# Row maxima turned by one transpose per phase, the image loop written out, and a 4-bit weight decoded inside the first image

## What is computed

```python
h = group_norm(x, 8 groups) * w + b
q, k, v = split(qkv_w @ h + qkv_b)             # one head of 128
x = x + proj_w @ (softmax(q k^T / sqrt(128)) v) + proj_b
t = tokens(x)                                  # 1024 x 128
n = layer_norm(t)
sq, sk, rq = n @ wq_s / 4, n @ wk_s, n @ wq_r / 4    # 8 heads of 16
retrieved = softmax(sq sk^T) @ (n @ wv_r)      # for each of 2 retrievers
t = t + mix(softmax(rq . (retrieved @ wk_ret)), retrieved) @ w_out
W4 = NF4_TABLE[qidx] * scales                  # 128 x 128, blocks of 16
t = t + layer_norm(t) @ W4^T @ W^T
```

## Time and profile before

| what | value |
|---|---|
| median of 3 runs | 4804.96 us (4800.92 to 4805.71) |
| profiled execution, its own time | 4802.95 us |
| its span (first to last instruction) | 4801.1 us |
| mean granted TensorE clock | 0.986 |
| instructions in it | 102107 |
| busy: PE, POOL, DVE, ACT | 96%, 88%, 81%, 69% |
| bytes moved by DMA | 191.77 MB, mean 40 GB/s |

### The profile page before, as it was taken

One profiled execution on the slowest core, in us unless ns is written; L12 is line 12 of the kernel. 1 busy time (PEld: TensorE's weight loads), 2 busy tenths in 40 slices (PEclk: granted clock), 3 DMA queues, 4 the chain that ended last, 5 costly groups with the idle time before them and its releaser, 6 DMA issues.

```text
span 4801.1 us, 102107 instructions
## 1 busy us (share of the span) xinstructions
PE 4608.7 (96%) x29838; PEld 2533.9 (53%) x29838; DVE 3906.7 (81%) x8190; ACT 3317.4 (69%) x6657; POOL 4242.2 (88%) x1142
## 2 busy tenths in 40 slices
PE   5899999999999999999999999999999999999985
PEld 4555555555555555555555555555555555555532
DVE  4788888888888888888888888888888888888863
ACT  2567777777777777777767777767777777777654
POOL 1589999999999999999999999999999999999996
PEclk9899999999999999999999999999999999999987
DMA  1011111111111111111111111111111111111010
GB/s 33 23 45 45 50 32 45 32 45 45 49 32 45 32 45 45 49 32 45 32 45 45 49 32 45 32 45 46 49 32 46 31 45 49 45 32 49 24 40 14
DMA packets 92739, 191.77 MB, mean 40 GB/s; under 512 B 16744, under 2 KB 50920, under 8 KB 92400
## 3 DMA queue, kind: packets, MB, share of 16 engines
q1 hardware_dynamic: 92400, 186.45, 13.9%
HBM read 17.53 MB, written 16.78 MB: 7 GB/s over the span
## 4 chain that ended last, share of the span: by engine, by line
PE 85%; DVE 6%; ACT 4%; issue 3%; POOL 1%; SPq 0%; DVEq 0%; ACTq 0%; DMA 0%; POOLq 0%
PE ps_u L804 18%; PE ps_bank L769 13%; PE ps_bank L791 11%; PE ps_bank L755 10%; PE ps_bank L741 4%; PE ps_bank L679 4%; DVE max_part L1067 4%; PE ps_bank L690 3%; PE ps_bank L710 3%; ACT p L962 3%; PE ps_bank L813 3%; PE ps_bank L743 3%; PE ps_bank L744 2%; PE ps_bank L742 2%; DVE max_part L1051 2%
## 5 line engine op out<-in xcount | busy, mean ns | idle before, releaser
L645 POOL TENSOR_TENSOR p_sum<-p_sum,p 128x2048 f32<-128x2048 f32 x768 | 3510.8, 4571 | 363.6 <-ACT p L962 316.6
L1067 DVE TENSOR_REDUCE max_part<-ps_bank 128x1 f32<-128x512 f32 x4096 | 2570.5, 683 | 513.0 <-PE ps_bank L769 500.8
L962 ACT ACTIVATE p<-ps_bank 128x512 f32<-128x512 f32 x4096 | 2153.3, 612 | 564.4 <-PE ps_bank L791 553.4
L804 PE MATMUL ps_u<-p,rv 128*32 128x512 f32 x8192 | 996.8, 604 | 3.2 <-ACT u_sb L968 2.5
L769 PE MATMUL ps_bank<-k_stack,q_stack 63*128 63x512 f32 x4096 | 863.5, 451 | 65.4 <-DVE max_part L1067 17.7
L791 PE MATMUL ps_bank<-q_stack,k_stack 64*128 64x512 f32 x4096 | 839.8, 449 | 35.2 <-ACT p L962 20.2
L791 PEld LDWEIGHTS ps_bank<-q_stack,k_stack 64*128 64x128 f32 x4096 | 372.0, 186 | 518.9 <-ACT p L962 177.0
L645 POOL TENSOR_TENSOR p_sum<-p 128x2048 f32<-128x2048 f32 x128 | 584.1, 4563 | 69.3 <-ACT p L962 69.3
L769 PEld LDWEIGHTS ps_bank<-k_stack,q_stack 63*128 63x128 f32 x4096 | 372.4, 185 | 507.6 <-DVE max_part L1067 199.2
L755 PE MATMUL ps_bank<-v,p 128*128 128x129 f32 x4096 | 498.9, 277 | 2.6 <-ACT p L919 1.6
L755 PEld LDWEIGHTS ps_bank<-v,p 128*128 128x128 f32 x4096 | 471.9, 191 | 38.1 <-DVE t_front L1097 12.5
(11 more groups left out here) (139 smaller groups left out, 4475.8 us busy)
## 6 DMA issues: line engine op xcount, KB each, us to landing
k_stack<-k_hi SPq DMA_DIRECT2D x256, 128.0 KB, 2.6
q_stack<-q_hi SPq DMA_DIRECT2D x256, 128.0 KB, 2.8
x_sb<-in_x SPq DMA_DIRECT2D x32, 512.0 KB, 3.6
k_stack<-k_lo SPq DMA_DIRECT2D x128, 128.0 KB, 2.6
q_stack<-q_lo SPq DMA_DIRECT2D x128, 128.0 KB, 2.8
t_held<-t_front SPq DMA_DIRECT2D x32, 512.0 KB, 2.9
rqk<-tok_next SPq DMA_DIRECT2D x32, 512.0 KB, 3.6
t_core<-t_held SPq DMA_DIRECT2D x32, 512.0 KB, 3.9
```

The source lines that it names most:

```text
L645: pool.tensor_tensor(p_sum[:, phase % 2, :, :], before, p1[:, step % ring, :, :], ALU.add)\
L804: last = pe.matmul(ps_u[n * QUAD:(n + 1) * QUAD, :], rv[:, key_tile, :], p1[:, step % ring, n, :], start=(key_tile == 0), stop=(key_tile = ...
L962: act.activation(p1[:, step % ring, n, :], bank_of("scores", index // 2, n % 2), ACT.Exp, scale=scale1)\
L1067: dve.tensor_reduce(max_part1[:, phase % 2, i, n, half:half + 1], bank_of("max1", index // 2, side), AXIS.X, ALU.max)\
```

## The change

- The maxima of a phase are turned by one transpose. `max1_last` writes its 16 columns in another order (head, then tile), the output has a row of 128 for each, ACT copies 16 x 128, and the DMA of `rows` lays them as before.
- In layer 0 likewise: one transpose, ACT copies 8 x 128 into a new tile `max_tile0`, and a new entry `row0` of SP lays it as the 1 x 1024 row.
- `in_order` writes every turn out; there is no loop.
- Set-up: x and the q/k/v weight go first on SP, eight weights, the codes and the scales on ACT's queue; two transposes run ahead of the rest; the set-up tiles lie in `p1`; the decode moves from set-up to behind `max0_last` of image 0, its product behind the last `value0` of image 0, its copy into `layer_norm_stats(0)`. PE's `values` and ACT's `scores` wait for it in every image.
- `load` is three images ahead, in the turn in which it used to be two ahead of the next.
- `mixed_channels` of half 0 waits for three `retrieve` stages, not two.
- All orders are new, with the same entries except those named; den.3 and evict_u.3 now stand at the end of the turn of their own image, not at the start of the next.

```diff
-load.0@2 rows.1@0 take_rqk.0@0 store.0@-1 rows.2@0 stack.0@1 take.0@0 rows.3@0 hold.0@1 rows.0@1 stack.1@1
+take_rqk.0@0 rows.1@0 take.0@0 rows.2@0 hold.0@1 stack.0@1 rows.3@0 load.0@3 store.0@-1 row0.0@2 rows.0@1
+stack.1@1
...
-scores.47@0/45 max0.6@2/20 max0.7@2/16 scores.48@0/43 scores.49@0/52 values.11@0 max_rows0.0@2/0 max_rows0.1@2/4
-scores.50@0/13 scores.51@0/65 max1.1@1/20 score0.0@2/4 max1.2@1/12 max1.3@1/36 score0.1@2/0 max1.4@1/54
...
+max_rows0.0@2/0 max1.2@1/64 scores.50@0/35 scores.51@0/01 max1.3@1/23 scores.52@0/56 max1.4@1/40 max1.5@1/21
+values.12@0 max1.6@1/35 max1.7@1/46 scores.53@0/02 den.2@0/1 max1.8@1/30 scores.54@0/52 turn_den.2@0/4
+scores.55@0/16 x_tokens.0@2/5 x_tokens.1@2/3 max1.9@1/24 max1.10@1/10 scores.56@0/65 values.13@0 scores.57@0/36
+max1.11@1/25 max1.12@1/41 max1.13@1/03 max1.14@1/26 score0.0@2/5 score0.1@2/4 score0.2@2/1 max1.15@1/05
...
-    for b in range(last + 1 - images, first):
-        turn_of(b)
-    before = links.count if links else 0
-    turn_of(first)
-    per_turn = links.count - before if links else 0
-    with nc.Fori(first + 1, last + 1, engines=[engine.engine], hint_back_edge=True) as b:
...
-    for b in range(last + 1, first + images):
+    for b in range(last + 1 - images, first + images):
         turn_of(b)
...
+                def row0(b, index):
+                    sp.wait_ge(max_tile0_ready, 1 * (b + 1))
+                    wait(sp, filled["score0"], halves * tiles * b)
+                    sp.dma_start(max_row0[0:1, :].bitcast(F32), max_tile0[:, :].bitcast(F32)).then_inc(row0_moved, 16)
...
-                        sp.dma_start(q_stack[ROWS - 1:2 * ROWS:ROWS, group * GROUP // 2 + pair,
-                                             half * HALF:(half + 1) * HALF].bitcast(F32),
-                                     max_row1[2 * pair:2 * pair + 2, :].bitcast(F32)).then_inc(rows_moved, 16)
+                        to = q_stack[ROWS - 1:2 * ROWS:ROWS, group * GROUP // 2 + pair, half * HALF:(half + 1) * HALF]
+                        heads = slice(2 * pair * tiles_per_half, 2 * (pair + 1) * tiles_per_half)
+                        sp.dma_start(to.bitcast(F32), max_row1[heads, :].bitcast(F32)).then_inc(rows_moved, 16)
...
-                    for i in range(tiles_per_half):
-                        last = pe.transpose(out[:, i * P:(i + 1) * P],
-                                            max_cols0[:, half * tiles_per_half + i:half * tiles_per_half + i + P], ident[:, :])
-                    last.then_inc(filled["max_rows0"], 1)
+                    pe.transpose(out[:, 0:P], max_cols0[:, 0:P], ident[:, :]).then_inc(filled["max_rows0"], 1)
...
-                        pe.wait_ge(max_row0_ready, halves * b + half + 1)
+                        pe.wait_ge(row0_moved, 16 * (b + 1))
...
+                    if b == 0 and query_tile == tiles - 1:
+                        pe.wait_ge(codes_decoded, 1)
+                        pe.matmul(ps_u[:, 0:P], lora, turned[:, 1, :], start=True, stop=True).then_inc(ffn_w_folded, 1)
...
-                    for i in range(tiles_per_half):
-                        last = pe.transpose(out[:, i * P:(i + 1) * P], max_cols1[:, GROUP * i:GROUP * i + P], ident[:, :])
-                    last.then_inc(filled["max_rows1"], 1)
+                    pe.transpose(out[:, 0:P], max_cols1[:, 0:P], ident[:, :]).then_inc(filled["max_rows1"], 1)
...
-                    act.copy(max_row0[0:QUAD, half * HALF:(half + 1) * HALF], bank_of("max_rows0", half)[0:QUAD, :])\
-                       .then_inc(max_row0_ready, 1)
+                    act.copy(max_tile0[:, :], bank_of("max_rows0", 0)[0:tiles, 0:P]).then_inc(max_tile0_ready, 1)
...
                     dve.tensor_reduce(max_cols0[:, 0:tiles], max_part0[:, :, :], AXIS.X, ALU.max, negate=True)\
                        .then_inc(max0_ready, 1)
+                    if b == 0:
+                        decode_ffn_weight()
...
-                        done = each if each == 16 else (half + 1) * each // halves
+                        done = each if each == 16 else each - 1 + half if name == "mixed_channels" else (half + 1) * each // halves
```

More of the change, by code:

```diff
@@ L37 @@
 PE_ORDER = """
[L38 to L52, removed]
@@ L63 @@
-scores.61@0/05 max_rows1.0@1/3 max1.17@1/14 values.14@0 max1.18@1/23 scores.62@0/16 scores.63@0/04 max1.19@1/52
-turn_u.2@0/1 scores.0@1/36 scores.1@1/05 values.15@0 score0.6@2/4 score0.7@2/3 scores.2@1/60 scores.3@1/25
-max1.20@1/14 value0.0@2/3 max1.21@1/60 max1.22@1/12 max1.23@1/45 value0.1@2/3 value0.2@2/6
+max1.24@0/01 scores.4@0/23 scores.5@0/45 turn_den.3@-1/6 turn_u.3@-1/0 value0.3@1/2 scores.6@0/16 max1.25@0/34
+values.0@0 max1.26@0/52 scores.7@0/16 mixed_channels.0@-1/0 mixed_channels.1@-1/3 max1.27@0/41 max1.28@0/56
@@ new lines @@
+values.1@0 max1.29@0/20 scores.8@0/34 scores.9@0/15 out1.0@-1/6 out1.1@-1/2 score0.8@1/3 max1.30@0/04
+scores.10@0/15 score0.9@1/6 score0.10@1/2 scores.11@0/31 max1.31@0/50 scores.12@0/64 score0.11@1/2
+scores.13@0/35 scores.14@0/10 max_rows1.1@0/6 values.2@0 scores.15@0/42 max1.32@0/36 max1.33@0/51 score0.12@1/0
+max1.34@0/34 max1.35@0/62 values.3@0 ln2_channels.0@-1/5 ln2_channels.1@-1/1 scores.16@0/34 scores.17@0/60
+scores.18@0/25 ffn.0@-1/1 ffn.1@-1/3 max1.36@0/46 scores.19@0/01 result.0@-1/2 score0.13@1/5 scores.20@0/30
@@ new lines @@
+max1.37@0/41 max1.38@0/62 values.4@0 max1.39@0/53 scores.21@0/40 max1.40@0/16 den.0@0/2 max1.41@0/54
+scores.22@0/30 turn_u.0@0/1 score0.14@1/2 scores.23@0/63 max1.42@0/50 norm_mean.0@2/4 score0.15@1/2
+scores.24@0/65 max1.43@0/40 turn_den.0@0/3 value0.4@1/2 scores.25@0/46 scores.26@0/35 values.5@0 scores.27@0/04
+max1.44@0/26 scores.28@0/35 value0.5@1/1 scores.29@0/02 max1.45@0/46 max1.46@0/35 values.6@0 scores.30@0/10
+scores.31@0/42 max1.47@0/63 norm_var.0@2/5 result.1@-1/1 max1.48@0/60 max1.49@0/43 max_rows1.2@0/1 value0.6@1/5
@@ L66 @@
+max1.20@1/45 value0.0@2/2 max1.21@1/36 max1.22@1/41 max1.23@1/50 value0.1@2/2 value0.2@2/3 den.3@0/6
 """
 ACT_ORDER = """
[L69 to L77, removed]
@@ new lines @@
+max_rows1.1@0 scores.27@0 scores.28@0 scores.29@0 ln2_apply.0@-1 scores.30@0 scores.31@0 ln2_apply.1@-1
+ln2_apply.2@-1 ln2_apply.3@-1 score0.12@1 evict_u.0@0 ln2_channels.0@-1 ln2_channels.1@-1 scores.32@0
+scores.33@0 scores.34@0 scores.35@0 scores.36@0 scores.37@0 scores.38@0 scores.39@0 result.0@-1 score0.13@1
+scores.40@0 scores.41@0 scores.42@0 scores.43@0 den.0@0 scores.44@0 scores.45@0 score0.14@1 scores.46@0
+norm_mean.0@2 scores.47@0 score0.15@1 scores.48@0 scores.49@0 scores.50@0 gate.0@0 scores.51@0 scores.52@0
@@ L112 @@
+value0.0@2 max1.42@1 max1.43@1 max1.44@1 max1.45@1 value0.1@2 max1.46@1 max1.47@1 value0.2@2
 """
@@ L612, in sync_program @@
                 in_order(nc, sp, order_of(SP_ORDER), images, {
-                    "load": load, "hold": hold, "take": take, "take_rqk": take_rqk, "stack": stack, "rows": rows,
+                    "load": load, "hold": hold, "take": take, "take_rqk": take_rqk, "stack": stack, "rows": rows, "row0": row0,
                     "store": store}, section=1)
```

202 lines of the change are left out of this document (107 added, 95 removed).

## The result

The changed kernel takes 4857.36 us (median of four runs, 4848.64 to 4867.88) against 4805.34 us for the kernel before (four runs): ratio 1.0110, 95% interval 1.0095 to 1.0124. Forecast was 4751 us. The sign was wrong, and the time lies outside the range.

What follows compares the result with a forecast made beforehand. PE, busy 96%, was taken as the bound; -59 + 9 - 9 + 5 = -54 us on 4802.95 gave 4749, adjusted to 4751 us because the median lay 2 us above; range 4698 to 4799.

Steps and rivals of the forecast that it cites:

- Part 2: Layer 0's row laid by a DMA behind load and store: score0.0 waits 0.3 us a turn, +9 us (bounds 0, +51).
- Rival (d): The row0 DMA wait before score0.0 replaces the transposes and eats the gain: 4832 at 3 us, up to 4865; chance 0.08.
- Part 1: One transpose on PE in place of four or eight: 1.98 us per image, -59 us (bounds -28 and -63).
- Part 3: Loop written out, removing sequencer waits at the den transposes: -9 us, with +14 on the other side.
- Part 4: Set-up and decode: image 0 starts 9.7 us earlier, but the decode delays its first value0: +5 us (bounds 0, +10).
- Part 5: New orders of all engines' stages: taken as 0, with 60 us allowed to either side.
- What would show it: Signs: norm_mean every 141.5 to 142.5 us; wrong above 143.5, below 141, or if row0's DMA leads PE's waits.

Runs made afterwards that it cites:

- experiment 3: The kernel before with nothing changed but the loop's turns written out: 4817.89 us, ratio 1.003.
- experiment 6: The changed kernel with row0 issued ahead of load and store and 19 idle transposes an image put back: 4848.94 us, ratio 1.0097.
- experiment 1: The changed kernel with row0 issued on SP ahead of load and store instead of behind them: 4785.89 us, ratio 0.9961.
- experiment 7: The changed kernel with row0 ahead of load and store, but issued only after both x_tokens additions: 4788.13 us, ratio 0.997.
- experiment 11: The changed kernel with row0 issued between load and store: 4793.51 us, ratio 0.9981.
- experiment 4: The kernel before with one transpose per phase of layer 1 and nothing else changed: 4800.79 us, ratio 0.9993.
- experiment 12: The kernel before with one transpose per phase of layer 1 and the last phase's rows issued ahead of the 512 KB take: 4786.36 us, ratio 0.9964.
- experiment 5: The changed kernel with row0 issued ahead of load and store and the hardware loop kept: 4778.95 us, ratio 0.9946.
- experiment 10: The changed kernel with the before kernel's orders, score0.0 and score0.1 moved later, row0 behind hold.0@1, and the hardware loop: 4884.13 us, ratio 1.0169.
- experiment 2: The changed kernel with the hardware loop of the kernel before put back: 4865.3 us, ratio 1.0121.
- experiment 9: The changed kernel, written out, with the before kernel's orders, score0.0 and score0.1 moved later, row0 behind hold.0@1: 4885.76 us, ratio 1.0173.
- experiment 8: The changed kernel with seven thrown-away 512-wide products on PE just before it waits for row0: 4837.83 us, ratio 1.0071.

## Why the prediction was wrong, step by step

The whole difference in one chain of medians, each step one pair of runs:

```
before                                   4805
loop written out           (3 - before)   +13
new orders, row0 DMA,
set-up, decode             (6 - 3)        +31   turns +41, ends -12 (profiled)
19 transposes gone         (1 - 6)        -63
row0 behind load and store (after - 1)    +71   of it clock: 20 to 39
after                                    4857
```

**The step that failed is Part 2**, the landing of row0. Its frame was right: row0 issued at 3.2 us (3.0 measured), score0.0 possible at 5.4 (5.3 in experiment 1), and a row landing between 5.2 and 7.1. In the 18 turns in which PE's wait ended with the row, it ended at 6.0 to 6.6 us, 6.5 at the median. I took the store's 2.7 us of the earlier trace rows for the whole way and wrote 0.3 us a turn; the pause was 1.36. But 2.7 us was the time of a store with nothing in front. Behind the load the store itself took 5.0 us, and row0 stood behind both. The wait lay inside the bound that I had put beside it, 1.7 us and +51 us, and I gave that bound little weight. Beyond it comes what the sum did not hold at all: the pause lets the granted clock fall to 0.57 to 0.63 in the 4 us behind it, in 22 of 28 turns. Per turn, the wait is 1.1 us (145.0 against 143.93) and the clock 1.4. Wait and clock together are 71 us in place of 9.

The Trainium skill (DMA: Bandwidth & Descriptors, Anatomy of one DMA) puts a fixed cost near 2 us on a DMA, by a fit on GpSimd's path; row0 goes through SP's queue. No run here times a 4 KB transfer with nothing in front. Experiment 7 bounds it: the row was there within 3.3 us of the end of its issue, which doesn't contradict the page. The row of the kernel after had 1 MB in front, and PE started 3.7 us after the end of its issue at the median.

**Rival (d)** named mechanism, place and threshold: PE before score0.0, once a turn, and the gain eaten from 2.1 us a turn. Its price was 4832 at 3 us. The measured wait, 1.36 us, was smaller than 2.1 and the result higher than 4832, since clock, orders and loop came on top. My reason against it, that one transfer's 3.6 us is largely latency and overlaps, holds for one transfer (experiment 11), not for two.

**Part 1** was right: -59 forecast, -63 measured (experiment 6 against 1). The transposes near the stretch where PE waits did count, in the new orders. In those of before, 12 transposes priced at 37 us brought 4 (experiment 4) and, with the rows issued earlier, 18 (experiment 12).

**Part 3** had the wrong sign: -9 forecast, +13 measured on the kernel before. The straight-code intervals of the earlier trace rows said it (+14), and I set them aside as filling. They were the right row. The Trainium skill (Runtime: NRT & Kernel Launch, Instruction fetch mechanics) explains why kernels prefer full unrolling: a taken branch can stall the fetch. A pause of that kind is seen: 20 of 28 turns of experiment 5, 1.5 to 2.2 us each, and 18 of experiment 10. But experiment 12, a loop too, has none in PE's list of waits. And written-out code lost 13 us on the old orders, could not be told from the loop on the new ones as shipped (experiment 2), and 7 us, within the intervals, lie between experiments 1 and 5. The measurement decides: here neither form wins by rule.

**Part 4.** Forecast: image 0 at 12.6, its maxima done at 36.6, a decode of 14.5 us, value0 at 67.2, +5 us. Measured: 15.5, 41.2, 5.9 us (41.07 to 47.17, with its cast), 62.95. Two errors. The start gained 6.8 us, not 9.7. Of the 2.9 us between, 2.0 are wk_ret: its eight DMAs are issued by 6.99 us, as I had it, but PE could start on it at 10.17, not 8.2 (the median from issue to landing went from 1.5 to 3.6 us). The rest lies on DVE, whose cast lasted 8.71 us, in place of 0.22, while POOL cleared k_stack and q_stack; the copy that PE waited for next stood behind it and began at 12.12, 0.8 us after PE's transposes had ended. And the decode's own 10.57 us in the earlier trace rows had run beside POOL's memsets; the same 15 comparisons alone took 2.12. I had carried over a duration stretched by a neighbour. The ends are 9 us shorter in the kernel after, 18.6 in experiment 1, where image 0's wait for row0 is gone too.

**Part 5**, orders at 0: between the same PE work in the same form, the turn grew by 1.46 us (6 against 3), 41 us, half of it waiting, most of that for ACT's exponentials. That lies inside the 60 I allowed, on the side that I did not choose. That it is the orders is the reading that is left, not shown by itself: experiments 9 and 10 were to isolate them and could not, and 12 does not decide it either; ACT's smaller copies and row0's DMA differ as well. The 0.73 us a turn of longer records has no cause that I can name.

**What would show it**, as forecast: the period "wrong above 143.5" read 146.41; PE's list of waits was led by the row0 DMA. Both signs were named, and both came.

## What to carry to other kernels

A small DMA that an engine waits for goes ahead of the large ones on its queue. Here one entry moved in an order turned 1.1% slower into 0.4% faster. The time of a transfer that ran with nothing in front of it (2.7 us) is not its time behind another (5.0 us). When a replaced wait is bounded by 0 and 1.7 us, price the upper end first, and add what a pause of that length does to the granted clock behind it. And before carrying a duration over to another place, look at what ran beside it.

If this change is wanted, row0 goes first. Experiment 5, with the loop kept, takes 4779 us against 4805 before and 4857 as changed; experiment 1, written out, takes 4786, and the two can't be told apart.

## What the runs showed of the hardware that I had not expected

- A pause of 1.36 us on the mean in a turn of 146 us was followed by a granted clock of 0.57 to 0.63 over 4 us in 22 of 28 turns. Six turns with pauses of 0.9 to 1.4 us kept the clock at 1.00. Seven products added into the pause made the kernel 20 us faster (experiment 8).
- A drop came behind two shorter waits as well: in experiment 9, 0.84 and 0.62 us, with 1.33 us of products between them, were followed by 0.63 over 4 us.
- 4 KB behind one transfer of 512 KB was there within 2.8 us of the end of its issue and cost PE nothing; behind two, PE started 3.7 us after that end at the median (experiment 11, the kernel after). A store of 512 KB took 2.7 us with nothing in front and 5.0 us right behind a load of 512 KB.
- DVE's 15 comparisons of 128x128 took 10.57 us beside POOL's memsets and 2.12 alone; one cast took 8.71 us while they ran. The Trainium skill (SBUF — State Buffer, SBUF: two separate sides) says that DVE in its two-port mode and GpSimd hold one pair of ports as an exclusive lock and the loser is blocked in full. The traces agree as far as they go: 2.1 us alone, 10.6 beside, and DVE's records end only behind the last of POOL's memsets, at 13.82 for 11.91 us before and at 11.98 for 11.89 us after. In which mode DVE ran they don't show.
- Writing the loop out cost 0.6 us a turn, in steps of about 0.1 us (experiment 3).
- The pause at the back edge depends on the code around it: 0.3 to 0.7 us before, 1.5 to 2.2 us in 20 of 28 turns with the new orders (experiment 5), 1.2 to 1.7 us in 18 turns of experiment 10, whose orders are nearly those of before.
